# An eight-batch, two-layer transformer on one core: stage places and zero products set anew, the maxima's rows of two pairs fetched in a batch of their own, and the second modulation pair made later

## The reference

```python
x = L0_attn_inputs                                   # 8 x 1024 x 128, float32
mod = (_silu(c) @ wmod).reshape(8, 6, 1, -1)         # sa, ca, ga, sb, cb, gb
ga = (2 * (ga >= 0) - 1) * jnp.maximum(jnp.abs(ga), 0.25)      # gb alike
h = _layernorm(x) * (1 + ca) + sa
x = x + ga * attention(h)
h = _layernorm(x) * (1 + cb) + sb
x = x + gb * feed_forward(h)
```

## Time and profile before

| | |
|---|---|
| median of 3 runs | 1708.97 us (1708.73 to 1711.44) |
| the profiled execution, own time | 1705.8 us |
| span in the trace | 1704.3 us |
| mean granted TensorE clock | 0.999 of full speed |
| TensorE, VectorE, ScalarE, GpSimd busy | 95%, 87%, 80%, 39% |
| first maxima product, first exp product | 124.6 us, 173.0 us |
| matrix products in the trace | 24168 |

### The profile page before, as it was taken

The page is one execution under the profiler, slowest core; times in us unless marked ns, Lnnn a source line. Parts: engine busy times, 40 slices in busy tenths (PEclk is TensorE's granted clock), DMA queues, the critical chain, the costliest instruction groups (busy, mean ns, idle before and its releaser), DMA issues.

```text
span 1704.3 us, 56706 instructions
## 1 busy us (share of the span) xinstructions
PE 1618.0 (95%) x24168; PEld 706.3 (41%) x24168; DVE 1479.7 (87%) x2259; ACT 1367.2 (80%) x1932; POOL 671.3 (39%) x1086
## 2 busy tenths in 40 slices
PE   7988999999999999999999999999999999999998
PEld 3754443344334443334334443334434443333335
DVE  5649988899889998899889998899989998999963
ACT  4442789988899878988899878988899888787785
POOL 2421435436443455435554365344554362102010
PEclk9999999999999999999999999999999999999999
DMA  2120201122120311112110311112110221101101
GB/s 74 52 75 18 69 28 54 32 60 62 53 63 23 94 57 55 30 43 76 58 60 19 94 43 55 46 47 78 43 57 24 70 61 41 55 24 54 36 26 35
DMA packets 83288, 87.22 MB, mean 51 GB/s; under 512 B 9452, under 2 KB 67484, under 8 KB 83036
## 3 DMA queue, kind: packets, MB, share of 16 engines
q1 hardware_dynamic: 82492, 83.07, 16.4%
q10 hardware_dynamic: 544, 0.52, 0.1%
HBM read 61.02 MB, written 21.99 MB: 49 GB/s over the span
## 4 chain that ended last, share of the span: by engine, by line
PE 61%; ACT 16%; DVE 14%; issue 4%; POOL 3%; DMA 2%; SPq 1%; ACTq 0%; POOLq 0%; DVEq 0%
PE pv_psum L812 20%; PE side_psum L537 15%; PE buffer L797 11%; ACT p L1039 11%; DVE row_max L1367 8%; PE buffer L787 7%; PE side_psum L630 2%; PE side_psum L597 1%; PE buffer L537 1%; PE pv_psum L822 1%; ACT o_sb L1048 1%; DVE st_f L1101 1%; ACT p0T L966 1%; ACT s L955 1%; POOL xn_f L1408 1%
## 5 line engine op out<-in xcount | busy, mean ns | idle before, releaser
L1367 DVE TENSOR_REDUCE row_max<-buffer 128x2 f32<-128x1024 f32 x1024 | 1219.5, 1217 | 117.7 <-PE buffer L787 105.8
L1039 ACT ACTIVATE p<-buffer 128x1024 f32<-128x1024 f32 x1024 | 1043.9, 1026 | 178.5 <-PE buffer L797 165.9
L812 PE MATMUL pv_psum<-p,v 128*9 128x256 f32 x8192 | 573.3, 381 | 4.4 <-ACT o_sb L1048 3.4
L787 PE MATMUL buffer<-k_ops,q_ops 24*128 24x512 f16 x2048 | 397.1, 385 | 29.8 <-ACT p L1039 21.7
L797 PE MATMUL buffer<-q_ops,k_ops 26*128 26x512 f16 x2048 | 396.5, 384 | 4.3 <-DVE row_max L1367 3.0
L812 PEld LDWEIGHTS pv_psum<-p,v 128*9 128x9 f32 x8192 | 154.9, 89 | 233.9 <-issue 148.6
L797 PEld LDWEIGHTS buffer<-q_ops,k_ops 26*128 26x128 f16 x2048 | 95.9, 91 | 349.6 <-issue 240.6
L787 PEld LDWEIGHTS buffer<-k_ops,q_ops 24*128 24x128 f16 x2048 | 96.0, 91 | 148.0 <-ACT p L1039 112.3
L1518 POOL TENSOR_SCALAR nm_parts<-nm 128x16 f16<-128x16 f32 x64 | 17.2, 268 | 348.5 <-DVE nm L1290 348.5
L1503 POOL TENSOR_TENSOR hm<-masks,hT_f 128x1024 f32<-128x1024 bf16 x56 | 120.0, 2148 | 63.5 <-PE side_psum L537 50.7
L537 PE MATMUL side_psum<-we,hm 128*32 128x128 f32 x3648 | 121.0, 274 | 0.0
(11 more groups left out here) (308 smaller groups left out, 1671.1 us busy)
## 6 DMA issues: line engine op xcount, KB each, us to landing
masks<-masks_rows SPq DMA_DIRECT2D x16, 1024.0 KB, 5.7
q_ops<-products SPq DMA_DIRECT2D x256, 48.0 KB
k_ops<-products SPq DMA_DIRECT2D x256, 48.0 KB
attention<-o_sb SPq DMA_DIRECT2D x248, 18.0 KB
x<-in_L_attn_inputs SPq DMA_DIRECT2D x8, 512.0 KB, 4.4
products<-q_parts SPq DMA_DIRECT2D x16, 256.0 KB, 2.2
w_sb<-in_L_ffn_W SPq DMA_DIRECT2D x16, 256.0 KB, 3.2
out<-x SPq DMA_DIRECT2D x16, 256.0 KB, 2.9
```

The lines of the kernel that those rows point to most:

```text
L787: m = e.matmul(buffer[:, hh, :], q_ops[rows, slot, of, i * P:(i + 1) * P], k_ops[rows, slot, of, halves(half)[1]], start=True, stop=True)
L812: m = e.matmul(pv_psum[q:q + VW, half * QUARTER:(half + 1) * QUARTER], v1[b % 2][:, kb, 2 * hp + hh, :], p_sb[n % KEPT][:, hh, part * QUAR ...
L1039: e.activation(p_sb[n % KEPT][:, :, :], unit("exp", n)[0][:, :, :], ACT.Exp, scale=over_scale[n // (2 * PERIOD)]).then_inc(S["exp_done"], 1)
L1367: e.tensor_reduce(mx[pair % 2][:, :, i, half], unit("max", n)[0][:, :, :], axis=AX.X, op=ALU.max).then_inc(S["max_done"], 1)
```

## The change

- `modulations(0, 1)`, the shift and scale of layer 0's second norm, moves on TensorE from `gate_products` and on VectorE from `gate_rows` to `weights_late`, into another bank. `gates` waits for the first pair's copy.
- `load_operands` of pairs 0 and 1 (`APART = 2`) issues the four fetches of the maxima's rows first, on semaphores of their own, then the four of the exp rows. Maxima products wait for the former, exp products for the latter. Later pairs are as before.
- The order of the front (`ALONE`), the places of some 100 stages in the 128 steps (`PLACES`), the table `COUNTED` with `SWITCH` and `LIGHT`, and both tables of zero products are set anew. The stages are the same, and so are those ahead of step -32. Zero products in the front go from 244 to 297, in the maxima stage from 141 to 159, in the steps from 0 on from 134 to 138 groups, at the end from 44 to 39.

```diff
+APART = 2
...
-SWITCH, LIGHT = 1.2, 6.6
+SWITCH, LIGHT = 0, 5.4
...
     def operands(g):
-        return S[f"operands{g % SLOTS}"], 8 * GROUP * 16 * (g // SLOTS + 1)
+        return S[f"operands{g % SLOTS}"], 8 * GROUP * 16 * (g // SLOTS + 1) - (4 * GROUP * 16 if g % SLOTS < APART else 0)
+
+    def max_operands(g):
+        return (S[f"max_rows{g}"], 4 * GROUP * 16) if g < APART else operands(g)
...
-    def fetch_operands(queue, g, w):
+    def fetch_operands(queue, g, w, first_rows, loaded_in):
...
-                for first_row in (MAX_ROWS, EXP_ROWS):
+                for first_row in first_rows:
...
             m.then_inc(S["gate_mm"], 1)
-            modulations(0, 1, psum[GATE_BANK])
...
             e.transpose(pv_psum[:, P:P + B * KC], b1_nat[:, :], ident[0:B * KC, 0:B * KC])
+            modulations(0, 1, pv_psum[:, 4 * B:])
...
             pe.wait_ge(S["gate"], 1)
+            pe.wait_ge(S["mod"], 1)
...
-            pe.wait_ge(*operands(pair // GROUP))
+            pe.wait_ge(*max_operands(pair // GROUP))
...
             pe.wait_ge(*maxima_in(pair))
+            pe.wait_ge(*operands(pair // GROUP))
...
             dve.wait_ge(S["zero_rows"], 4)
-            modulations(0, psum[GATE_BANK], 2)
...
             dve.wait_ge(S["b1T"], 1)
+            modulations(0, pv_psum[:, 4 * B:], 2)
...
                     sp.wait_ge(*operands(g))
+                    sp.wait_ge(*max_operands(g))
...
-                fetch_operands(e, g, w)
+                if g < APART:
+                    fetch_operands(e, g, w, (MAX_ROWS,), S[f"max_rows{g}"])
+                else:
+                    fetch_operands(e, g, w, (MAX_ROWS, EXP_ROWS), S[f"operands{g % SLOTS}"])
+            if g < APART:
+                for w in range(2):
+                    fetch_operands(e, g, w, (EXP_ROWS,), S[f"operands{g}"])
```

On VectorE the order around the powers was `index 0 1 1, powers 0, onehot 0 1`, and is `index 0 1 1, over_gating 0 0, onehot 0 1, hm 0 2, powers 0`. On ScalarE `gating 0 0 0` stood behind both halves of `transpose_p 0 7` and now stands ahead of them. At the end of `ALONE`, which ScalarE follows too:

```diff
-moe_a 0 7, parts 0 1 0, residual 0 1, moe 0 7, transpose_p 1 0 0, scores 1 2 0, stats 0 2 1 0, times_v 1 0, stats 0 2 1 1, transpose_p 1 1 0, channels
-0 2 1, apply 0 2 1, softmax 1 2, qk1 0 0 1, v1 0 1, qk1 0 1 1, parts 0 0 1, exp0 1 2, parts 0 1 1, scores 1 3 0, sums0 1 0, transpose_p 1 2 0"""
...
+moe 0 7, hm 0 7, softmax 1 1, scores 1 2 0, v1 0 0, channels 0 2 1, transpose_p 1 1 0, parts 0 0 0, parts 0 1 0, residual 0 1, qk1 0 0 1, stats 0 2 1
+0, times_v 1 0, qk1 0 1 1, stats 0 2 1 1, exp0 1 2, scores 1 3 0, softmax 1 2, exp0 1 3, times_v 1 1, apply 0 2 1, v1 0 1, parts 0 0 1, scores 1 4 0,
+parts 0 1 1"""
```

More of the change, by code:

```diff
@@ L110 @@
 PLACES = """
[L111 to L118, removed]
@@ L123 @@
[L123 to L130, removed]
@@ new lines @@
+-151 stats 0 1 0 1, -151 apply 0 1 0, -144 channels 0 1 0, -142 wg 0 0, -142 top 0 0 0, -142 top 0 0 1, -142 index 0 0 0, -141 index 0 0 1, -136
+gating 0 0 0, -139 onehot 0 0, -133 gating 0 0 1, -133 onehotT 0 0, -124 over_gating 0 0, -137 masks_out 0 0, -127 masks_load 0 0, -126 hm 0 0, -123
+hm 0 1, -121 moe_a 0 0, -120 moe 0 0, -123 hm 0 2, -116 moe_a 0 1, -115 moe 0 1, -118 hm 0 3, -112 moe_a 0 2, -111 moe 0 2, -107 moe_a 0 3, -106 moe 0
+3, -107 residual 0 0, -100 stats 0 2 0 0, -98 stats 0 2 0 1, -98 apply 0 2 0, -93 channels 0 2 0, -91 qk1 0 0 0, -60 parts 0 0 0, -88 qk1 0 1 0, -72
@@ L177 @@
-exp0 0 7, stats 1 0 0 0, stats 1 0 0 1, wg 0 0, transpose_p 0 7 0, top 0 0 0, stats 1 0 1 0, transpose_p 0 7 1, gating 0 0 0, top 0 0 1, stats 1 0 1
-1, index 0 0 0, squares 0, apply 1 0 0, index 0 0 1, times_v 0 7, onehot 0 0, up 0 1, stats 0 1 1 0, gating 0 0 1, stats 0 1 1 1, onehotT 0 0,
-channels 0 1 1, channels 1 0 0, apply 0 1 1, wg 0 1, hm 0 0, limits 0, top 0 1 0, apply 1 0 1, channels 1 0 1, moe_a 0 0, g0 1 0, masks_out 0 0,
-gating 0 1 0, inverse 0, g0 1 1, onehotT 0 1, gating 0 1 1, over_gating 0 0, index 0 1 0, moe 0 0, masks_load 0 0, top 0 1 1, hm 0 1, moe_a 0 1, index
@@ L181 @@
-0 1 1, powers 0, later 1, onehot 0 1, moe 0 1, hm 0 2, hm 0 3, residual 0 0, masks_out 0 1, moe_a 0 2, moe 0 2, masks_load 0 1, moe_a 0 3, moe 0 3,
-scores 1 0 0, v0 1, stats 0 2 0 0, gates 1, moe_a 0 4, moe 0 4, hm 0 4, stats 0 2 0 1, hm 0 5, hm 0 6, moe_a 0 5, exp0 1 0, channels 0 2 0, qk1 0 0 0,
-over_gating 0 1, moe 0 5, apply 0 2 0, moe_a 0 6, softmax 1 0, moe 0 6, qk1 0 1 0, scores 1 1 0, exp0 1 1, parts 0 0 0, hm 0 7, softmax 1 1, v1 0 0,
-moe_a 0 7, parts 0 1 0, residual 0 1, moe 0 7, transpose_p 1 0 0, scores 1 2 0, stats 0 2 1 0, times_v 1 0, stats 0 2 1 1, transpose_p 1 1 0, channels
@@ L185 @@
[L185 removed]
+apply 0 0 1, channels 0 0 0, channels 0 0 1, softmax 0 0, g0 0 0, v0 0, scores 0 0 0, scores 0 1 0, softmax 0 1, exp0 0 0, g0 0 1, scores 0 2 0, exp0
+0 1, transpose_p 0 0 0, transpose_p 0 1 0, stats 0 0 1 0, later 0, stats 0 0 0 0, scores 0 3 0, exp0 0 2, gates 0, scores 0 4 0, scores 0 4 1,
+transpose_p 0 2 0, exp0 0 3, times_v 0 0, scores 0 5 0, times_v 0 1, scores 0 5 1, softmax 0 2, exp0 0 4, transpose_p 0 3 0, times_v 0 2, softmax 0 3,
@@ new lines @@
+softmax 0 4, softmax 0 5, transpose_p 0 3 1, scores 0 6 0, transpose_p 0 4 0, exp0 0 5, scores 0 6 1, times_v 0 3, stats 0 0 1 1, softmax 0 6,
+transpose_p 0 4 1, stats 0 0 0 1, transpose_p 0 5 0, sums0 0 0, up 0 0, transpose_p 0 5 1, scores 0 7 0, stats 0 1 0 0, apply 0 0 0, stats 0 1 0 1,
+times_v 0 4, apply 0 1 0, stats 1 0 0 0, exp0 0 6, softmax 0 7, scores 0 7 1, channels 0 1 0, transpose_p 0 6 0, wg 0 0, transpose_p 0 6 1, masks_out
+0 0, top 0 0 0, stats 1 0 0 1, exp0 0 7, top 0 0 1, times_v 0 5, stats 1 0 1 0, index 0 0 0, gating 0 0 0, transpose_p 0 7 0, stats 1 0 1 1,
@@ new lines @@
+transpose_p 0 7 1, squares 0, sums0 0 1, apply 1 0 0, index 0 0 1, gating 0 0 1, times_v 0 6, onehot 0 0, times_v 0 7, up 0 1, onehotT 0 0, channels 0
+1 1, channels 1 0 0, stats 0 1 1 0, stats 0 1 1 1, apply 0 1 1, limits 0, apply 1 0 1, wg 0 1, inverse 0, channels 1 0 1, g0 1 0, top 0 1 0, hm 0 0,
+g0 1 1, index 0 1 0, top 0 1 1, scores 1 0 0, gating 0 1 0, gating 0 1 1, hm 0 1, moe_a 0 0, index 0 1 1, over_gating 0 0, onehot 0 1, moe 0 0,
+onehotT 0 1, hm 0 2, powers 0, moe_a 0 1, moe 0 1, moe_a 0 2, hm 0 3, moe 0 2, gates 1, moe_a 0 3, masks_load 0 0, moe 0 3, v0 1, moe_a 0 4,
@@ new lines @@
+over_gating 0 1, hm 0 4, moe 0 4, later 1, masks_out 0 1, moe_a 0 5, channels 0 2 0, residual 0 0, moe 0 5, stats 0 2 0 0, stats 0 2 0 1, masks_load 0
+1, exp0 1 0, moe_a 0 6, moe 0 6, hm 0 5, scores 1 1 0, transpose_p 1 0 0, qk1 0 0 0, apply 0 2 0, moe_a 0 7, exp0 1 1, hm 0 6, softmax 1 0, qk1 0 1 0,
+moe 0 7, hm 0 7, softmax 1 1, scores 1 2 0, v1 0 0, channels 0 2 1, transpose_p 1 1 0, parts 0 0 0, parts 0 1 0, residual 0 1, qk1 0 0 1, stats 0 2 1
+0, times_v 1 0, qk1 0 1 1, stats 0 2 1 1, exp0 1 2, scores 1 3 0, softmax 1 2, exp0 1 3, times_v 1 1, apply 0 2 1, v1 0 1, parts 0 0 1, scores 1 4 0,
```

36 lines of the change are left out of this document (21 added, 15 removed), and 36 rows, old and new, of tables (COUNTED, ZEROS_AHEAD, ZEROS_BESIDE).

## The result

The changed kernel takes 1728.81 us (median of 6 runs, 1724.14 to 1731.19), the kernel before 1708.85 (6 runs). The ratio is 1.0113, 95% interval 1.0103 to 1.0124. Forecast were 1699.7 and a range of 1690 to 1711. The change makes this kernel 1.1% slower, and the prediction has both the sign and the size wrong.

What follows compares the result with a forecast made beforehand. TensorE bounds a steady batch, busy 188.6 of 195 us. Gains of 4.0 (front), 0.3 (fetches), 3.6 (steady batches) and 1.4 (end) make 9.3 us, from 1708.97 to 1699.7; own range 1693 to 1705, with the other cases 1690 to 1711.

Steps and rivals of the forecast that it cites:

- Steady batches: Six batches: two TensorE waits at `transpose_p` 6 and 7 vanish, 3.6 us less; other moved stages 0; ends -19 and +9.
- The +9: Upper end for the steady batches: three new waits of 0.5 us in each of six batches.
- Rival 2: Steady batches get longer: ScalarE's p late at replanned steps, five waits per batch, 14 us, 1713.7 us; chance 0.13.
- Front up to the experts' end: Stages up to `moe 0 7`: modulation, new order and earlier GpSimd sums bring it 4.0 us earlier; ends 0 and 6.
- Second modulation pair late: Front: gates start some 1.2 us earlier, needing only the gate products; net gain 0.5 us, ends 0 and 1.2.
- Maxima's rows fetched ahead: Ahead of the first maximum: rows fetched first, but ScalarE's late store holds them; -0.3 us, ends -1.5 and +2.6.
- Maxima stage: Steps -32 to -1: VectorE has the same stages, so 48.4 us stay; 18 more zero products, 2.1 us, hidden.
- End: Last two batches: 24 fewer steps carry a single group of value products, 1.4 us less.

Runs made afterwards that it cites:

- e1: The changed kernel with `sums_load` put back from step 138 to 132, all else as changed: 1704.95 us, ratio 0.9979 to the kernel before.
- e7: The changed kernel with `sums_load` at 132 and value products planned by the old costs (COUNTED, SWITCH, LIGHT): 1715.49 us, ratio 1.0045.
- e9: The kernel before with only the two code edits (second modulation pair late, maxima's rows fetched ahead), no table changed: 1705.21 us, ratio 0.9980.
- e8: The changed kernel with `sums_load` at 132 and ScalarE's store of k's second half put ahead of batch 1's third exponential, as before: 1708.02 us.
- e10: The changed kernel with `sums_load` at 132 and the first pairs' rows fetched together as before (`APART = 0`): 1711.71 us, ratio 1.0016.
- e5: The changed kernel with `sums_load` moved from step 138 to 135: 1706.96 us, ratio 0.9986 to the kernel before.
- e12: The changed kernel with `sums_load` left at 138 and the second half's masks' store and load put behind it in SP's queue: 1705.73 us.
- e3: The changed kernel with twelve zero products put behind step 17 of batches 1 to 6, where TensorE stood idle: 1723.89 us, ratio 1.0095.
- e2: The kernel before with only the six places of the sums as changed (load at 138, reciprocal at 143): 1734.53 us, ratio 1.0156.
- e4: The changed code, order and places up to step -1, with the old batches from step 0 on: 1708.91 us, ratio 1.0001 to the kernel before.
- e6: The changed kernel with `sums_load` left at 138 and the reciprocal `sums` put from step 143 to 146: 1740.70 us, ratio 1.0178.

## Why the prediction was wrong, point by point

**Steady batches** is the step that failed. It set the moved stages at 0 ("meet no wait of size") after naming four, and the sums' six moves are not in it at all. By the prediction's own manner the step had to count what `sums_load` is moved past on SP. The rows for it stood in the trace of before: the load at 570.10, eight fetches, a store at 578.17 that is not free to go, a load of masks at 581.02. Behind those the load goes out 19.9 us into the batch instead of 9.7, lands beside the 1 MB of masks in 6.3 us instead of 2.5, and is there 3 us after VectorE has reached the reciprocal. In place of 0 for this move, in a step of -3.6, the runs showed +21.4 in steps 16 to 23 of six batches (changed kernel against e1). The +9 that I allowed above it was made of three waits of 0.5; one wait of 3 on an engine that is 91% busy (178.0 of 195) was not in it. VectorE has 17 us of slack in a batch and recovers none of these 3: TensorE, with 6.4 idle, has to stop too, because its banks are emptied by VectorE.

**Its other parts** held better. With the load back, batches 1 to 5 are 0.3, 1.0, 0.5, 0.2 and 0.4 us shorter than before; I had 0.6. (The number of value groups changes at 21 steps of a steady batch, not 28, and single groups fall from 112 to 90 in the last two, not to 88; both traces bear this out. The term for the end would have been 1.3 instead of 1.4.) Rival 2 had the right sign and 0.13, but its mechanism, ScalarE's late p at the replanned steps, is not what happened: e7 shows that the replanned numbers save time with these places. That the sign came true is luck.

**Front up to the experts' end** was right: the first softmax starts at 18.26 (18 to 19 forecast), the last Relu of the experts at 96.54 instead of 101.05, 4.5 us earlier (4.0 forecast), and `channels 0 2 0` waits 0.32. The first maximum is at 122.25, and I had 120 to 121. What I did not see is that it is not this chain that ends last ahead of the maxima. TensorE's list now holds `times_v 1 1` and `scores 1 4 0` there, and e9, without the new order, has its first maximum at 121.54, the changed kernel at 122.25. At the last Relu the changed kernel is 2.5 us ahead of e9 (99.02), at the first maximum 0.7 behind: the order's gain is used up in TensorE's list, whose last wait is 0.49 us for p0T.

**Second modulation pair late**: in e9 the gates start at 13.04 instead of 13.84, 0.8 us earlier (1.2 forecast), and the last Relu is 2.0 earlier (0.5 forecast at that point). How much of that is chance one execution can't tell: in the kernels with this edit the gates start between 12.51 and 13.61. **Maxima's rows fetched ahead** was mis-sized: 0.3 forecast, with the store as what limits it. The store went out 3.8 us behind the split (4 to 5 forecast) and does not limit the first maximum (e8); the fetch is worth 6 us behind this order (e10). In e9 it takes 1.1 us of the 3.1 at the first maximum, since the wait of 1.50 is gone. My prediction weighed the Trainium skill's "DMA: Bandwidth & Descriptors", section "Rules for kernel authors", that a second issuing engine only saves issue time, and made 1.5 us of it at most. In e8, where ScalarE still issues the store but early, nothing is gained; with SP as the issuer it was not run. The same section says to issue a transfer early and to wait for it late; by it the six steps of `sums_load` were what to look at, and e1 agrees with 23 us, though by e5 and e12 the place in the queue counts and not the six steps.

**Maxima stage** was to stay at 48.4 us; it takes 50.09, and 48.78 against 46.80 when both run at the full clock. **End**: -1.4 forecast; the last two batches are 2.0 and 1.4 us longer than before in e1 and 6.8 and 1.9 in the changed kernel. Part of that is the clock, which falls there at 1466.5, 1558.6 and 1640.6 behind waits below 1 us. It fell in the last two batches in all runs with the new places there, in e7 (which has the value products of before in these two batches) and e3 only once, twice in e2 with the old places, and in the profiles of before, e4 and e9 not at all ahead of the last 6 us. Whether the new value products or the zero products bring that on stays open. That the profiled execution of e4 is 2.0 us shorter in span than that of before, at the same median, says little: it ran at a mean clock of 1.000 and is the second fastest of ten (1703.99 to 1710.80), and one run of the kernel before beside it, also at 1.000, took 1703.37.

## What to carry to other kernels

When a transfer is moved in an order, list what stands ahead of it in its issuing engine's queue before and after: not the steps it moves count, but the waits that it moves behind and the large transfers that it then shares the DMA engines with. Then follow its user's chain to the end, for moving the user away from the wait (e6) can put the same wait on a dearer engine. And a plan that is fitted as a whole is tested by undoing one number at a time: here one number of the tables cost 23 us and hid that the rest, with the two edits of code, was 0.2% faster than before, which the two edits of code are by themselves (e9).
